# First x in one transfer at the head of SyncE's queue, ids by GpSimd's queue, and warm-up products divided 11 + 9 around the spreading of the ids

## The reference

```python
# step 1: attention pooling under a mask that the type selects
attn_in = tanh(x @ W1 + b1)                  # W1 [512, 128]
scores  = attn_in @ v                        # one score per token
p       = softmax(where(mask[type], scores, -1e30))
x       = x + (p @ x) / count(mask)
# step 2: a linear layer whose weights the category selects
x       = x + x @ W[cat] + b[cat]            # W [64, 512, 512]
```

## Time and profile before

| | |
|---|---|
| time, median of 3 runs | 308.31 us (308.03 to 309.88) |
| time of the profiled execution | 308.65 us |
| its span, first to last instruction | 306.9 us |
| TensorE, busy | 301.0 us (98%) |
| VectorE, busy | 278.0 us (91%) |
| ScalarE, busy | 262.6 us (86%) |
| GpSimd, busy | 85.6 us (28%) |
| moved by DMA | 105.69 MB, mean 344 GB/s |

### The profile page before, as it was taken

How to read it: one execution, slowest core, us unless ns; L and a number is a source line. 1 busy time by engine, 2 the same in 40 slices (tenths; PEclk the granted TensorE clock), 3 DMA queues, 4 the chain that set the end, 5 groups by cost and what they waited for, 6 DMA issues and landing times.

```text
span 306.9 us, 4890 instructions
## 1 busy us (share of the span) xinstructions
PE 301.0 (98%) x1284; PEld 233.0 (76%) x1284; DVE 278.0 (91%) x385; ACT 262.6 (86%) x429; POOL 85.6 (28%) x119
## 2 busy tenths in 40 slices
PE   8999999999999999999999999999999999999995
PEld 4445488788887878878787887878788787888884
DVE  4447998999999999999999999999999999999961
ACT  2265889989899998999999899999989999898942
POOL 5120302224341233425223341421434132202000
PEclk9999999999999999999999999999999999999999
DMA  7999999999999999899999999999999999986133
GB/s 264 412 388 414 390 400 398 373 418 356 392 347 359 386 314 420 305 395 355 378 366 309 413 351 360 358 344 386 331 407 347 357 378 326 402 315 219 70 136 137
DMA packets 23516, 105.69 MB, mean 344 GB/s; under 512 B 2625, under 2 KB 2626, under 8 KB 13378
## 3 DMA queue, kind: packets, MB, share of 16 engines
q1 hardware_dynamic: 23058, 103.03, 89.2%
q10 hardware_dynamic: 432, 2.36, 1.9%
HBM read 88.61 MB, written 16.78 MB: 343 GB/s over the span
## 4 chain that ended last, share of the span: by engine, by line
PE 88%; issue 5%; DMA 2%; DVE 2%; POOLq 1%; ACT 1%; POOL 1%; ACTq 0%
PE ps_y L682 17%; PE ps_y L684 17%; PE ps_y L683 17%; PE ps_pre L641 13%; PE ps_y L694 5%; PE ps_y L695 5%; PE ps_y L696 5%; PE ps_y L700 4%; PE ps_pT L658 2%; DMA w_raw<-in_L_cond_W 2%; PE ps_y L670 1%; PE ps_scores L651 1%; PE ps_scores L649 1%; DVE w_lo L484 1%; POOLq L293 1%
## 5 line engine op out<-in xcount | busy, mean ns | idle before, releaser
L484 DVE TENSOR_TENSOR w_lo<-w_raw,w_hi 128x2048 fp32r<-128x2048 f32 x58 | 134.9, 2326 | 0.0
L351 ACT ACTIVATE w_hi<-w_raw 128x2048 fp32r<-128x2048 f32 x58 | 111.7, 1927 | 9.1 <-POOL w_raw L287 7.4
L682 PE MATMUL ps_y<-w_hi,xT_hi 128*128 128x512 f32 x232 | 91.7, 395 | 0.0
L684 PE MATMUL ps_y<-w_hi,xT_lo 128*128 128x512 f32 x232 | 90.5, 390 | 0.0
L683 PE MATMUL ps_y<-w_lo,xT_hi 128*128 128x512 f32 x232 | 90.3, 389 | 0.0
L287 POOL TENSOR_TENSOR w_raw<-w_raw,ident 128x512 f32<-128x512 f32 x26 | 33.6, 1294 | 113.0 <-DVE w_lo L484 74.5
L684 PEld LDWEIGHTS ps_y<-w_hi,xT_lo 128*128 128x128 f32 x232 | 43.5, 188 | 9.4
L683 PEld LDWEIGHTS ps_y<-w_lo,xT_hi 128*128 128x128 f32 x232 | 43.6, 188 | 8.8
L682 PEld LDWEIGHTS ps_y<-w_hi,xT_hi 128*128 128x128 f32 x232 | 43.6, 188 | 8.6
L512 DVE TENSOR_TENSOR z_lo<-ps_y,z_hi 128x512 fp32r<-128x512 f32 x64 | 43.6, 682 | 7.2 <-ACT z_hi L387 7.2
L387 ACT ACTIVATE z_hi<-ps_y 128x512 fp32r<-128x512 f32 x64 | 38.8, 606 | 9.7 <-PE ps_y L684 5.1
(11 more groups left out here) (70 smaller groups left out, 363.5 us busy)
## 6 DMA issues: line engine op xcount, KB each, us to landing
w_raw<-in_L_cond_W SPq DMA_DIRECT2D x62, 1024.0 KB, 8.4
out<-out_sb SPq DMA_DIRECT2D x64, 256.0 KB, 6.0
x_raw<-in_x SPq DMA_DIRECT2D x15, 1024.0 KB, 7.0
out_sb<-in_L_cond_b SPq DMA_DIRECT2D x16, 256.0 KB, 5.4
w_raw<-in_L_cond_W ACTq DMA_DIRECT2D x2, 1024.0 KB, 6.3
x_raw<-in_x SPq DMA_DIRECT2D x2, 512.0 KB, 4.8
w_pack<-in_W_b_v ACTq DMA_DIRECT2D x1, 257.0 KB, 2.8
b_raw<-in_L_cond_b SPq DMA_DIRECT2D x2, 128.0 KB, 8.7
```

The source lines that it names most:

```text
L351: nc.scalar.activation(w_hi[k % NH][:], w_raw[k % NW][:], ACT.Copy).then_inc(w_hi_ready, 1)
L484: nc.vector.tensor_tensor(w_lo[k % NL][:], w_raw[k % NW][:], w_hi[k % NH][:].bitcast(F32), ALU.subtract).then_inc(w_lo_ready, 1)
L682: nc.tensor.matmul(y[:], xT_hi[q][:, c, xs], w_hi[k % NH][:, c, :], start=(c == 0), stop=False)
L684: last = nc.tensor.matmul(y[:], xT_lo[q][:, c, xs], w_hi[k % NH][:, c, :], start=False, stop=(c == DC - 1))
```

## The change

SyncE's first instruction is now the load of the whole first x, 1 MB in one transfer, with one semaphore `x0_in`. The load of `ids_row` is issued by GpSimd, ahead of its clearing of `ident`. `hidden_raw(0)` waits for all of x before its first product. TensorE runs 11 products on zeros before the ids are spread and 9 after, where it was 9 and 10.

```diff
-        x0_in = [sem(f"x0_in{h}") for h in range(2)]
+        x0_in = sem("x0_in")
...
-            sp.dma_start(ids_row[:], ids.rearrange("(a n) -> a n", a=1)).then_inc(ids_in, 16)
-            for h, c in enumerate(halves):
-                sp.dma_start(x_raw[0][:, c, :], xg[0][:, c, :]).then_inc(x0_in[h], 16)
+            sp.dma_start(x_raw[0][:], xg[0]).then_inc(x0_in, 16)
             sp.wait_ge(ids_in, 16)
...
+            pool.dma_start(ids_row[:], ids.rearrange("(a n) -> a n", a=1)).then_inc(ids_in, 16)
             nc.gpsimd.memset(ident[:], 0.0).then_inc(pool_step, 1)
...
                 if g == 0:
                     pe.wait_ge(w1_in, 16)
+                    pe.wait_ge(x0_in, 16)
...
-                    if g == 0 and c % HALF == 0:
-                        pe.wait_ge(x0_in[c // HALF], 16)
...
             pe.wait_ge(warm_ready, 1)
-            warm_up(9)
+            warm_up(11)
             pe.wait_ge(ones_ready, 2)
             pe.wait_ge(ids_bf_ready, 1)
...
-            warm_up(10)
+            warm_up(9)
             hidden_raw(0)
```

## The result

The kernel became slower: 312.38 us (median of 6 runs, 311.10 to 314.11) against 308.25 us (6 runs, 307.88 to 309.88). The ratio is 1.0124 with a 95% interval of 1.009 to 1.0158, which is 2.8 to 4.9 us. The profiled execution took 312.93 us at a span of 311.1 us, 4.3 us more in both than before. The forecast was 308.0 us, 307.3 to 308.9.

A forecast was written before the change was run, and what follows sets the result against it. A stream of loads starting with W 0 was taken as the bound; W 0 at 9.0 instead of 9.3 us takes 0.3 us off the profiled 308.65, and the median's 0.34 us lower level gives 308.0 us, range 307.3 to 308.9.

The forecast's parts named there:

- Ids by GpSimd: Step at the kernel's start: ids loaded by GpSimd are in at 3.2 us, between bounds of 2.1 and 4.6 us.
- L: Time at which the ids are in at the kernel's start: 2.77 us before, forecast 3.2 us.
- L + 5.8: Landing of W 0 if the ids bound it: 0.9 us to issue plus 4.9 us to land, forecast 9.0 us.
- GpSimd is late: Rival, chance 0.20: late ids delay the issue of W 0, DMA engines run empty before it, end 308.5 to 309.5 us.
- X + 2.5: Landing of W 0 if x bounds it, 2.5 us after all of x is in (X, forecast 6.1): 8.6 us.
- nothing moves: Rival, chance 0.20: x stays near 6.8 us because the DMA engines' slow first stretch sets it; end 308.3 us.
- The clock: Rival, chance 0.03: TensorE idles between warm-up parts, its clock falls to 1.2 GHz, `hidden_raw(0)` doubles from 3.4 us; end 310.3 us.
- the stream of loads: Loads from the first W to that of 31.1 us, claimed to set VectorE, TensorE's start at 58.71 us and the end.
- one for one: Claim that any shift of the first loads passes whole to the W of 31.1 us, VectorE, 58.71 us and the end.
- VectorE's pause before 31 us: Sign: VectorE's 1.34 us wait for a W, ending at 31.12 us, should follow the first W and end at 30.8 us.
- 1.02 us to spare: TensorE's slack from its pauses before 38.41 and 58.71 us, 0.37 + 0.65 us, claimed to hide a later TensorE start.
- Its timeline has no pause between 31.12 us and that `xT_lo`: Claim that VectorE works without waiting from 31.12 us to `xT_lo` at 56.33 us, for which TensorE waits until 58.71 us.

The follow-up runs named there:

- experiment 1: Changed kernel with the ids back at the head of SyncE's queue, x whole and warm-up 11 + 9 kept: 308.58 us against 309.1, ratio 0.9985.
- experiment 4: Kernel before without any products on zeros: 309.4 us against 308.58, ratio 1.0027.
- experiment 7: Ids at the head of ScalarE's queue: changed kernel (x whole) 308.43 us, kernel before (x in halves) 308.96 us, against 308.58.
- experiment 3: Changed kernel with 32 instead of 11 products on zeros ahead of the spreading of the ids: 312.38 us against 309.1, ratio 1.0108.
- experiment 8: Changed kernel run again unaltered: 313.89 us against 308.58 for the kernel before, ratio 1.018.
- experiment 5: Changed kernel, x or x and `w1_pack` issued after the ids; kernel before, GpSimd's ids, second half of x after them: `ids_bf` at 3.76, 3.10, 5.56 us.
- experiment 2: Kernel before with only the ids moved to GpSimd, x in halves, warm-up 9 + 10: 312.97 us against 309.1, ratio 1.0132.

## Why the prediction was wrong

**The step that failed** is "Ids by GpSimd": L = 3.2 us, upper bound 4.6. It was 6.7. As a price of GpSimd's load by itself 3.2 us was right (3.08 with nothing ahead), but in part by luck: that load began only at 1.29 us and took 1.8 us, where the sum had 0.75 + 0.42 us and SyncE's 2.02 us, and SyncE's own load took 1.3 us in experiments 1 and 4. Missing was the same effect that the prediction used earlier for W 0, that a transfer comes in behind the bytes ahead of it. The ids had been the first issue on their queue with only `w1_pack` beside them; the change put 1.31 MB in front, which at the rates of the earlier trace rows (275, then 418 GB/s) takes till 6 us. The late ids moved the loads behind them: W 0 landed 5.7 us after the ids, where the prediction had L + 5.8, and at 12.4 us. The rival "GpSimd is late" had the right side and, with the engines empty ahead of W 0, part of the mechanism, but its bound was taken from how instructions stretch, not from the queue, and it ended at 309.4 us.

**"X + 2.5".** The whole x came at 6.3 us (predicted 6.1). But with x sooner, W 0 did not come sooner: in experiment 1 x was in at 6.2 us and W 0 at 9.1 us, X + 2.9; in experiment 7, x whole, at 5.7 and 9.2 us, X + 3.5, and the sum had left out `w1_pack`, which had moved from 3.5 to 6.3 us, since x no longer came after it. The three loads ahead of VectorE's first work on W 0 are the same bytes in any order, and it began at 9.16 and 9.19 us there, 9.30 before. So the rival "nothing moves" was right on W 0, for another reason than the one it gave: the order of bytes changed, not their sum.

**The clock.** The rival was there at 0.03, with the argument that the clock is 1.00 in every window. That was a misreading. The products on zeros in the earlier trace rows took 0.23 us each; the same ones took 1.16 / 9 = 0.13 us in experiment 3 once TensorE had worked through, so those of the start ran at 1.2 GHz and the column was not to be trusted. The clock did not fall in the changed kernel; its first rise came late. As the rival said, `hidden_raw(0)` lengthened, by 1.8 us, and by 1.0 us in experiment 8 (forecast 3.4). That the clock can fall, too, as the rival feared, shows in one run of experiment 5, that with nothing ahead of the ids. TensorE had worked from 1.08 to 5.85 us and then stood still for 2.87 us; the window from 9.4 to 12.7 us (columns as in the earlier trace rows) reads 0.50, where that of the changed kernel from 9.2 to 12.9 us reads 1.00, though its pieces took as long:

```profile
9.40:12.70 3.30, 3.30 (x6) 1.24 (x5) 1.42 (x3) 0.00 (x0) 0.43 (x2) 0.50 1.01 427
9.20:12.90 3.70, 3.70 (x6) 1.60 (x6) 1.18 (x4) 0.46 (x1) 2.18 (x6) 1.00 0.97 401
```

**What carried to the end.** The prediction had one way only, the stream of loads, "one for one", and called itself wrong if VectorE's pause before 31 us did not follow the first W. That came true: the pause is gone in the changed kernel (experiment 3 shows the row; in experiment 8 0.94 of 1.34 us is left), whose chain goes over TensorE. "One for one" is not shown for experiment 3 either: W 0 came 3.0 us later there and the end 3.3 us, but within 1.6 to 5.1, which also fits TensorE's lateness less its spare time, 3.0 − 1.0 = 2.0 us; and the W of the earlier trace rows came 4.7 us later. "1.02 us to spare" fits as a number (experiment 4). For the changed kernel TensorE's own way gives 4.6 − 1.0 = 3.6 us and the stream 3.1 us; measured were 2.8 to 4.9 us, and by its timeline hardly anything was absorbed (TensorE was 4.6 us late at 14.47 us and 4.33 at 63.04 us, where its pause had grown from 0.65 to 1.16 us). How far the clock matters once the ids are late is not settled: with the slow clock the loss was 4.1 us (the changed kernel) and 3.9 (experiment 2), without it 3.3, and the intervals overlap.

**A row that was overlooked.** "Its timeline has no pause between 31.12 us and that `xT_lo`" was false. The kernel before has one more, in which VectorE waits for a W that SyncE issued only at 38.21 us, when TensorE's product with the W of that buffer was done:

```profile
47.27 0.69 DVE L471 TENSOR_TENSOR w_raw<-w_raw,ident 128x512 f32<-128x512 f32 x1 [0.84 <-DMA w_raw<-in_L_cond_W]
```

In the changed kernel the same row reads:

```profile
51.01 0.69 DVE L473 TENSOR_TENSOR w_raw<-w_raw,ident 128x512 f32<-128x512 f32 x1 [1.44 <-DMA w_raw<-in_L_cond_W]
```

So the stream is not rigid to the end: from here on TensorE's products decide when loads are issued. That the spare time still came out at 1 us in experiment 4 does not prove the account; it is one figure that fits.

**Hidden edits.** `hidden_raw(0)` waiting for all of x and the other split of the warm-up cost nothing, as said (experiment 1: 0.9985). GpSimd's later setup was in no run without late ids, so its price is not measured. It came more than forecast: the clearings 1.2 us later (0.4 to 1.0 was said) and the mask copies at 8.52 instead of 4.61 us, as they need the ids. VectorE's first instruction that uses a mask waited for TensorE, in both kernels. The products on zeros behind the ids, 9 here and 10 before, cost only with late ids: they ran from 7.25 to 9.35 us while x and `w1_pack` had been in since 6.5 us, and they stand in the chain.

## What to carry to other kernels

A small load on which other loads depend has to be issued before the large ones, or at the same moment at the head of another queue (experiment 7): here half a microsecond behind 1.3 MB made 512 bytes 3.9 us late, though the instruction took 0.65 us. When bytes already fill the DMA engines, an earlier place for one transfer is a later one for another that the same instruction needs; add up the bytes before each consumer. And when a rule explains one wait of a profile, apply it to every transfer that the change touches.

## What the runs showed of the hardware

- The 512 bytes passed no data that had been issued some 0.5 us before them: `ids_bf` began at 3.10, 3.76, 5.56 and 6.70 us with 0, 0.26, 0.79 and 1.31 MB ahead, by GpSimd's queue. By SyncE's queue behind x it was 6.07 us, by ScalarE's behind `w1_pack` 6.43 us, at the head of SyncE's or ScalarE's 2.0 to 2.8 us.
- Large loads did the same across the two hardware queues. `w1_pack`, issued 0.57 us after x, moved only from 4.9 us on, when x was nearly through (experiment 7); W 0, issued at 2.90 us, moved nothing before 5.3 us (experiment 1). Issued at the same moment, x and `w1_pack` moved side by side (128 and 114 packets between 1.8 and 5.6 us), and `w1_pack` took 5.7 instead of 2.8 us. The Trainium skill (DMA: Bandwidth & Descriptors, Queues, rings and completion order) says that each DMA engine serves its queues in turn, a packet at a time. The loads issued together agree. Those issued 0.57 us and more behind x, the ids among them, do not follow from taking turns alone; why they wait is open.
- GpSimd's load began at 1.28 or 1.29 us in every kernel that had it, after 0.82 us of idleness, which is when VectorE's last clearing ended. The Trainium skill (SBUF — State Buffer, SBUF: two separate sides) has GpSimd kept from writing descriptors while VectorE holds the port. The time fits; but no run here moved the clearings or shows that they hold the port, so it is not shown.
- TensorE's clock column showed 1.00 from the first microsecond in the kernels before and after, while f32 pieces of the changed kernel took 0.85 us instead of 0.43; it read 0.50 at the same pace only in the run where the clock had been up before. The pieces were at full pace from 5.64 us where TensorE had worked since 1.07 us. In the changed kernel, where it had stood still from 3.6 to 7.06 us, a piece begun at 11.70 us still took the long time. With the clock up, TensorE stood still for 0.91 and 1.72 us before `hidden_raw(0)` in experiment 7 and kept its pace (3.70 us); after 2.87 us the clock fell (experiment 5).
